# Chunk 0 of the causal attention moved into the last two steps of the memory block, and the causal block's first lead-in step dropped

## The reference, cut to what matters

```
xn = layernorm(x)                        # per token, 128 features
q, k = xn Wq + bq, xn Wk + bk            # 64 wide
A = softmax(q k^T / 8, masked to the past, inside the chunk)
x = x + A (xn (Wv Wo)) + (bv Wo + bo)    # Wv and Wo are joined into one 128 x 128 table
xn = layernorm(x); e = argmax(xn Wg + bg)
x = x + gelu(xn W1[e] + b1[e]) W2[e] + b2[e]
```

## Time and profile before

| what | value |
|---|---|
| median of three runs | 1473.49 us (1465.39 to 1476.33) |
| profiled execution, its own time | 1473.16 us |
| its span in the profile | 1471.4 us |
| TensorE busy | 1297.2 us (88% of the span) |
| VectorE, ScalarE, GpSimd busy | 1006.7, 787.0, 526.5 us |
| memory block, last two steps | 929.0 to 981.9 us of the span |
| causal block, steps -2 and -1 | 981.9 to 1026.8 us |
| causal block, from step 0 on | 1026.8 to 1239.0 us |

### The profile page before, as it was taken

One profiled execution on the slowest core, in us unless ns is written; L12 is line 12 of the kernel. 1 busy time (PEld: TensorE's weight loads), 2 busy tenths in 40 slices (PEclk: granted clock), 3 DMA queues, 4 the chain that ended last, 5 costly groups with the idle time before them and its releaser, 6 DMA issues. The chain is left out here.

```text
span 1471.4 us, 23007 instructions
## 1 busy us (share of the span) xinstructions
PE 1297.2 (88%) x7338; PEld 772.9 (53%) x7338; DVE 1006.7 (68%) x2761; ACT 787.0 (53%) x1593; POOL 526.5 (36%) x688
## 2 busy tenths in 40 slices
PE   4899999999999899944779998988999998999898
PEld 1223333333333789922355555667667676777533
DVE  7688888888885666647867876334575654666586
ACT  1377677777776205545546664223554544466555
POOL 3433443453312215258434444331221212533056
PEclk7799999999999899967889999999999999999999
DMA  5211211111111622210122234202111312000001
GB/s 151 71 35 45 56 34 45 56 48 31 56 34 52 157 47 70 55 38 23 30 65 59 60 75 99 59 13 87 62 66 63 122 59 86 9 1 2 1 22 36
DMA packets 80059, 80.05 MB, mean 54 GB/s; under 512 B 19835, under 2 KB 63947, under 8 KB 79939
## 3 DMA queue, kind: packets, MB, share of 16 engines
q1 hardware_dynamic: 76639, 72.95, 18.2%
q0 software_dynamic: 2272, 4.66, 1.4%
q10 hardware_dynamic: 1028, 0.98, 0.2%
HBM read 63.21 MB, written 13.85 MB: 52 GB/s over the span
## 5 line engine op out<-in xcount | busy, mean ns | idle before, releaser
L706 DVE TENSOR_REDUCE a_nm<-a_aps 128x1 f32<-128x512 f32 x512 | 330.0, 686 | 74.5 <-PE a_aps L426 74.5
L666 ACT ACTIVATE a_prob<-a_sps 128x512 f32<-128x512 f32 x512 | 270.0, 599 | 121.2 <-PE a_sps L439 120.7
L426 PE MATMUL a_aps<-a_K,a_Q 96*128 96x512 bf16 x512 | 190.2, 397 | 28.5 <-DMA a_K<-k_parts 27.0
L439 PE MATMUL a_sps<-a_Q,a_K 99*128 99x512 bf16 x512 | 155.9, 384 | 1.3 <-ACT a_prob L666 1.3
L1540 POOL TENSOR_TENSOR p_h<-p_sl,p_t 128x512 f32<-128x512 f32 x72 | 102.3, 1428 | 150.0 <-ACT p_sl L1744 96.9
L449 PE MATMUL a_ops<-a_prob,a_Vg 128*32 128x512 f32 x1024 | 136.9, 608 | 0.0
L426 PEld LDWEIGHTS a_aps<-a_K,a_Q 96*128 96x128 bf16 x512 | 50.3, 98 | 153.7 <-DVE a_nm L706 90.0
L2353 POOL TENSOR_TENSOR c_h<-c_h,c_G 128x512 f32<-128x512 f32 x24 | 31.9, 1334 | 171.8 <-DMA c_G<-choice_rows 128.0
L1599 PE MATMUL p_up_a<-x_normT,p1w_w 128*128 128x512 f32 x144 | 78.6, 629 | 14.5 <-ACT p_sl L1744 12.2
L104 POOL CAST a_ms<-a_mr 16x128 bf16<-16x128 f32 x32 | 9.0, 280 | 228.8 <-ACT a_mr L623 228.8
L1744 ACT ACTIVATE p_sl<-p_up_a 128x512 f32<-128x512 f32 x72 | 42.2, 592 | 77.1 <-PE p_up_b L1601 76.8
(11 more groups left out here) (649 smaller groups left out, 2742.1 us busy)
## 6 DMA issues: line engine op xcount, KB each, us to landing
c_G<-choice_rows SPq DMA_DIRECT2D x32, 512.0 KB, 5.8
p_G<-gates_by_expert SPq DMA_DIRECT2D x30, 512.0 KB, 7.6
a_Q<-q_parts SPq DMA_DIRECT2D x192, 32.0 KB
a_K<-k_parts SPq DMA_DIRECT2D x31, 96.0 KB
q_parts<-a_partsq SPq DMA_DIRECT2D x7, 384.0 KB, 2.8
k_parts<-a_partsk SPq DMA_DIRECT2D x7, 384.0 KB, 2.8
token_outputs<-m0e_y SPq DMA_DIRECT2D x39, 64.0 KB, 1.5
m0w_w<-in_L_ffn_W SPq DMA_DIRECT2D x1, 2048.0 KB, 8.6
```

The lines of the kernel that those rows point to most:

```text
L426: nc.tensor.matmul(aps[n % 3][:, :], Q[0:MAX, head, q * P:(q + 1) * P], K[0:MAX, head, :], start=True, stop=True).then_inc(a_ready, 1)
L439: nc.tensor.matmul(sps[(NS * u + k) % 3][:, :], K[0:KB, head, q * P:(q + 1) * P], Q[0:KB, head, :], start=True, stop=True).then_inc(s_read ...
L666: nc.scalar.activation(prob[u % 2][:, j, q, :], sps[n % 3][:, :], ACT.Exp).then_inc(p_done, 1)
L706: nc.vector.tensor_reduce(nm[u % 2][:, s:s + 1], aps[n % 3][:, :], AX.X, ALU.max, negate=True).then_inc(a_used, 1)
```

## The change

The start and the end of the attention of causal chunk 0 are written a second time as functions `head_*` inside the memory block, on buffers that its last two steps no longer use. In step 6: the normalisation (DVE, before j=1), its transposes (PE, behind j=1), queries and keys (j=3), the joined table, values and the joined bias (j=5), the scores behind the last pair and ahead of the `down` products, then maxima and exponentials. In step 7: the transposes of the probabilities behind j=0, the weighted sum behind j=4, the addition to the residual at j=6 and the statistics at j=8. SP issues the eight loads of attention weights in its turn for chunk 6, and ACT issues the move of the keys. POOL makes the mask and adds the bias. The tables that later chunks need live in a new object `CausalHead` that both blocks hold (four tables in the buffer that was `xn20`, so it takes the place of one).

In the causal block the steps -2 and -1 are replaced by one written-out lead-in that does the first half of chunk 1 and the second half of chunk 0's choice of experts, with 10, 4, 8 and 24 `keep_busy` matmuls where there were 10, 4, 13, 12, 8, 16, 4 and 12. Semaphores that chunk 0 would have raised are raised by hand at the start. The memory block's ScalarE ends on a load of the square-root table. From step 0 on the order of every engine is what it was. Lines left out of the diff are the loads of the other weights, the same removal in the other engines, and parameters that name the PSUM bank.

```diff
-def memory_and_swiglu(nc, net, d, mw, place, ys, rows):
+class CausalHead:
...
+        p = Scope(nc, ctx, "ch")
+        self.tables = p.sb("tables", [P, TC, D])
+        self.wqk, self.wvo, self.bc, self.mask = (self.tables[:, i, :] for i in range(TC))
+        self.qkb, self.qks = p.sb("qkb", [P, 1]), p.sb("qks", [P, 1])
...
+        xn1, xn2 = [rows, p.sb("xn11", [P, TC, D])], [head.tables, p.sb("xn21", [P, TC, D])]
...
+        hb = (ops, bps, cps)
+        xnh, xch, qkh, kTh, Vh = rz[1], l[1], az[1], sn[0], sn[1]
+        prob_of = {0: cn[0][:, 0:P], 2: cn[0][:, P:4 * P], 1: cn[1][:, 0:2 * P], 3: k[:, :]}
+        PTh = [content, cc, cs, csum]
+        wvh, woh, boh, bvh = az[0][:, 0:H], az[0][0:H, P:2 * P], az[0][:, 2 * P:3 * P], az[0][0:H, 3 * P:3 * P + 1]
+        bvbh, wvTh = rz[0][0:H, 0:P], rz[0][0:H, P:2 * P]
...
+                if c == B - 2:
+                    sp.wait_ge(x2_turned, B - 1)
+                    sp.wait_ge(phi_done, B - 1)
+                    sp.wait_ge(h_set, 2)
+                    ca = lambda n: d[f"L2_attn_{n}"]
...
+                    sp.dma_start(head.qkb[H:2 * H, :], col(ca("bk"))).then_inc(h_loaded, 16)
+                    sp.dma_start(wvh, ca("wv")).then_inc(h_loaded, 16)
+                    sp.dma_start(woh, ca("wo")).then_inc(h_loaded, 16)
+                    sp.dma_start(bvh, col(ca("bv"))).then_inc(h_loaded, 16)
+                    sp.dma_start(boh, row(ca("bo")).to_broadcast([P, D])).then_inc(h_loaded, 16)
 
...
+                    pool.wait_ge(x2_turned, B - 1)
+                    nc.gpsimd.memset(head.mask[:, :], 0.0).then_inc(h_set, 1)
+                    pool.wait_ge(h_set, 3)
+                    nc.gpsimd.affine_select(out=head.mask[:, :], in_=head.mask[:, :], compare_op=ALU.is_ge, fill=-1e11,
+                                            base=0, pattern=[[-1, P]], channel_multiplier=1).then_inc(mask_made, 1)
+                if s == B - 2:
+                    pool.wait_ge(bias_done, 1)
+                    pool.wait_ge(hx_done, 1)
+                    xt = net.x[:, 0:TC, :]
+                    nc.gpsimd.tensor_tensor(xt, xt, over_tiles(head.bc[:, :], TC), ALU.add).then_inc(hx_biased, 1)
...
+            def head_turn():
+                pe.wait_ge(r_done, B)
+                pe.wait_ge(hx_done, 1)
+                for i in range(TC):
+                    last = nc.tensor.transpose(bps[:, htok(i)], xnh[:, htok(i)], net.ident[:, :])
+                last.then_inc(hx_turned, 1)
+
+            def head_turn_values():
+                pe.wait_ge(h_loaded, 16 * head.LOADS)
+                nc.tensor.transpose(cps[0:H, 0:P], wvh, net.ident[:, :]).then_inc(wv_turned, 1)
...
+
+            def head_queries_and_keys():
+                pe.wait_ge(hxc_done, 1)
+                nc.tensor.matmul(bps[:, :], head.wqk[:, :], xch[:, :], start=True, stop=True).then_inc(hqk_ready, 1)
+
+            def head_join():
+                pe.wait_ge(wvT_done, 1)
+                nc.tensor.matmul(cps[:, P:2 * P], wvTh, woh, start=True, stop=True).then_inc(wvo_ready, 1)
+
...
+                pe.wait_ge(wvo_done, 1)
+                for i in range(TC):
+                    last = nc.tensor.matmul(cps[:, htok(i)], xch[:, htok(i)], head.wvo[:, :], start=True, stop=True)
+                last.then_inc(V_ready, 1)
+
+            def head_bias():
+                pe.wait_ge(bvb_done, 1)
+                pe.wait_ge(hqk_done, 1)
+                nc.tensor.matmul(bps[:, 0:D], bvbh, woh, start=True, stop=True).then_inc(bias_ready, 1)
+
+            def head_scores():
+                pe.wait_ge(hk_moved, 16)
+                pe.wait_ge(V_done, 1)
+                pe.wait_ge(bias_done, 1)
...
+                for q in SCORE_ORDER:
+                    bank, off = SCORE_PLACE[q]
+                    n = (q + 1) * P
+                    nc.tensor.matmul(hb[bank][:, off:off + n], qkh[0:H, q * P:n], kTh[0:H, 0:n],
+                                     start=True, stop=True).then_inc(s_ready, 1)
+
+            def head_turn_prob():
+                pe.wait_ge(p_done, 1)
+                for i in range(TC):
+                    bank, off = TURN_PLACE[i]
+                    for q in range(i, TC):
+                        last = nc.tensor.transpose(hb[bank][:, off + (q - i) * P:off + (q - i + 1) * P],
+                                                   prob_of[q][:, htok(i)], net.ident[:, :])
+                last.then_inc(p_turned, 1)
+
+            def head_weigh():
+                pe.wait_ge(PT_done, 1)
+                for q in range(TC):
+                    for i in range(q + 1):
+                        last = nc.tensor.matmul(ops[:, htok(q)], PTh[i][:, htok(q - i)], Vh[:, htok(i)],
+                                                start=(i == 0), stop=(i == q))
+                last.then_inc(w_ready, 1)
 
             join_tables()
...
+                    if s == B - 2:
+                        if j == 1:
+                            head_turn()
+                            head_turn_values()
+                        if j == 3:
+                            head_queries_and_keys()
+                            head_join()
+                        if j == 5:
+                            head_values()
+                            head_bias()
+                    if s == B - 1:
+                        if j == 0:
+                            head_turn_prob()
+                        if j == 4:
+                            head_weigh()
+                if s == B - 2:
+                    head_scores()
                 middle(s)
...
+                    if s + 2 == B - 1:
+                        nc.scalar.activation(stdh, net.stat[:, 0:TC, 1], ACT.Sqrt, bias=net.epst[:, 0:1]).then_inc(h_rooted, 1)
...
+                act.wait_ge(r_done, B)
+                nc.scalar.activation(xch[:, :], bps[:, :], ACT.Copy).then_inc(hxc_done, 1)
+                act.wait_ge(wv_turned, 1)
+                nc.scalar.activation(wvTh, cps[0:H, 0:P], ACT.Copy).then_inc(wvT_done, 1)
+
+            def head_queries_and_keys():
+                act.wait_ge(hqk_ready, 1)
+                act.wait_ge(b_scaled, 1)
+                nc.scalar.activation(qkh[:, :], bps[:, :], ACT.Identity, scale=head.qks[:, :], bias=head.qkb[:, :]).then_inc(hqk_done, 1)
+                act.wait_ge(hqk_done, 1)
+                act.dma_start(kTh[0:H, :], qkh[H:2 * H, :]).then_inc(hk_moved, 16)
+                act.wait_ge(wvo_ready, 1)
+                nc.scalar.activation(head.wvo[:, :], cps[:, P:2 * P], ACT.Copy).then_inc(wvo_done, 1)
...
+                nc.scalar.activation(Vh[:, :], cps[:, :], ACT.Copy).then_inc(V_done, 1)
+
+            def head_exponentials():
+                nc.scalar.preload_act_table(ACT.Exp)
+                act.wait_ge(nb_done, 1)
+                for q in SCORE_ORDER:
...
+                    last = nc.scalar.activation(prob_of[q], hb[bank][:, off:off + (q + 1) * P], ACT.Exp,
+                                                bias=nbh[:, q:q + 1], accum_out=sumsh[:, q:q + 1])
+                last.then_inc(p_done, 1)
+                nc.scalar.preload_act_table(ACT.Silu)
...
+                    if s == B - 2:
+                        if j == 2:
+                            head_tokens()
+                        if j == 4:
+                            head_queries_and_keys()
+                        if j == 6:
+                            head_values()
                 middle(s)
+                if s == B - 2:
+                    head_exponentials()
+            nc.scalar.preload_act_table(ACT.Sqrt)
...
+                v.wait_ge(h_rooted, 1)
+                nc.vector.reciprocal(stdh, stdh)
+                v.drain()
+                for i in range(TC):
+                    last = ts(xnh[:, htok(i)], net.x[:, i, :], net.stat[:, i, 0:1], stdh[:, i:i + 1], ALU.subtract, ALU.mult)
+                last.then_inc(hx_done, 1)
...
+            def head_biases():
+                v.wait_ge(h_loaded, 16 * head.LOADS)
+                tt(head.qkb[:, :], head.qkb[:, :], head.qks[:, :], ALU.mult).then_inc(b_scaled, 1)
+                nc.vector.tensor_copy(bvbh, bvh.to_broadcast([H, P])).then_inc(bvb_done, 1)
...
+                    v.wait_ge(s_ready, (1, 3, 3, 4)[i])
+                    dg = hb[bank][:, off + q * P:off + (q + 1) * P]
+                    tt(dg, dg, head.mask[:, :], ALU.add)
+                v.drain()
+                for q in SCORE_ORDER:
+                    bank, off = SCORE_PLACE[q]
+                    last = nc.vector.tensor_reduce(nbh[:, q:q + 1], hb[bank][:, off:off + (q + 1) * P], AX.X, ALU.max,
+                                                   negate=True)
+                last.then_inc(nb_done, 1)
+
+            def head_copy_prob(which):
+                v.wait_ge(p_turned, 1)
+                for i in which:
+                    bank, off = TURN_PLACE[i]
...
+                    last.then_inc(PT_done, 1)
+
+            def head_add():
+                v.wait_ge(p_done, 1)
```

(114 more changed lines are left out.)

186 lines of the change are left out of this document (87 added, 99 removed).

## The result

The changed kernel takes 1456.93 us, the median of 20 runs (1451.85 to 1463.59), against 1472.26 us for the kernel before in 20 runs of its own (1462.37 to 1476.33). The ratio is 0.9902, 95% interval 0.9887 to 0.9917, so 14.4 us faster (12.2 to 16.6). The profiled execution took 1460.11 us.

The account below looks back on a forecast made before the run. TensorE was taken to bound the kernel, busy 88% of the span, with the lead-in set by one chunk's latency. 1473.2 + 8.5 (memory block) - 21.5 (lead-in) = 1460.2 us, given as 1460, range 1454 to 1466.

Parts of the forecast that it names:

- Work added to TensorE: Memory steps 6 and 7: 7.78 us of moved work plus a 0.7 us wait, ending the block 8.5 us later.
- The wait: Step 6: `head_values` on TensorE waits for the joined table that ScalarE copies, 0.5 to 1.0 us, taken as 0.7.
- the joined table and the joined bias: Step 6, TensorE: one matmul each at a quarter of the four value matmuls' 0.99 us, 0.50 us together.
- The scores: End of step 6: 2.35 us on TensorE, standing where it now waits 0.83 us, so 1.52 us is added.
- The lead-in: From the engines' meeting to `weigh` of chunk 1: 23.4 us where it was 44.88, so 21.5 us earlier.
- The semaphore increments: Start of the lead-in: six on TensorE, between 0 and 0.6 us, taken as 0.3.
- The count of 24: Lead-in: 24 `keep_busy` end at 20.3 us, probabilities are ready at 19.4, so the count decides by 0.9 us.
- The clock at step 0: Under `weigh`: the low clock stays, leaving the sum unchanged; the high one would return 2.2 us.
- The first rival: Step 0: the clock stays at 2.4 GHz into it, giving 1458.0 us; chance 30%.
- longer stall: Step 6: TensorE waits 2.8 us and falls to the low clock, 2.5 us more, giving 1465.5 us; chance 9%.
- the expert weights and choices: After the lead-in: they land late, about 3 us if transfers do not overlap, giving 1463 us; chance 7%.
- VectorE and POOL did collide: Steps 6 and 7: collisions cost 1.06 us per added VectorE instruction, 1481 us if all paid; chance 4%.

Follow-up runs that it names:

- a_kb12: The changed kernel with 12 instead of 24 `keep_busy` ahead of `turn_prob` of chunk 1; 0.9903 of the kernel before.
- c_memory_only: The changed memory block with the causal block of the kernel before, so chunk 0's attention is computed twice; 1.0052 of the kernel before.
- b_fill: The kernel before with 19 instead of 12 `keep_busy` ahead of the second `turn_prob`, filling the idle 1.46 us; 0.9981 of the kernel before.

## Why the prediction was right

The forecast was 13 us faster (1460 against 1473.2) and the measurement 14.4. The mechanism, TensorE time paid in steps 6 and 7 against latency returned in the lead-in, is what the rows show. The closeness is in part luck: the two main terms came out 0.8 and 0.6 us less favourable than forecast, and the clock, on which I chose wrongly, gave 2.6 us. The terms:

- **Work added to TensorE.** 8.5 us were forecast, 9.3 measured, outside my 8.3 to 8.8. The wait was right: 0.7 forecast, 0.69 from start to start. What I sized too low are the matmuls with 64 rows, the joined table and the joined bias: 0.41 us each where I took a quarter of four value matmuls, 0.25, and the pair behind each starts its second matmul 0.1 us later (934.49 to 935.45). Queries and keys took 0.96 instead of 0.86, values 1.09 instead of 0.99. Another 0.2 us lie between the last `down` products and the meeting of the engines (11.70 instead of 11.51 us); what takes them is not shown. The scores took the place of the wait, as said. The joined table could have been read instead of guessed, since the kernel before has the same matmul in its lead-in, 0.39 us from start to start:
```profile
990.59 0.46 PE L2395 MATMUL c_ups<-c_wo,c_wvT 64*128 64x128 f32 x2 [1.01 <-ACT c_wvT L2544]
990.98 3.17 PE L75 MATMUL c_hps<-ident 128*128 128x128 f32 x26
```
- **The lead-in.** 21.5 us were forecast, 20.9 measured in the profiled pair. The semaphore increments took 0.9 us where I took 0.3. The count of 24 decided over the chain, by 1.1 us (the last exponential ended at about 1007.8, and with 12 counts the transposes came 1.05 us earlier), where I had 0.9.
- **The clock at step 0.** Here the choice was wrong in its value: I took the low clock, and all seven profiled executions with the changed lead-in or a variant of it show the high one. The first rival, 1458.0 us, is the case that came; it priced the high clock at 2.2 us, and step 0 was 2.6 us shorter, since the first pair behind `weigh` ran faster too. The reason I gave, the length of the gap, is not the cause: with both gaps the high clock came in three of three executions of `a_kb12` and `c_memory_only`, and in one of five of the kernel before. The rule of the Trainium skill that I weighed there (page "TensorE: Matmul & The Clock Gate", section "Part 4: PE-mode transpose"), that transposes don't count for the clock, is neither shown nor refuted: 3.0 us without a matmul, transposes in them, did not lower it.
- **What gain is the kernel's own.** With the same clock on both sides, a rise in the same place (4.61 us) and the high clock under `weigh`, the stretch takes 126.21 us in `b_fill`, whose filled gap does not move `weigh`, and 114.61 us in the changed kernel: 11.6 us. That is the 20.9 us of the lead-in less the 9.3 us of steps 6 and 7. With the low clock before and the high one after it is 14.2 us. The five executions of the kernel before average 128.1 us, the two of the changed kernel 114.6: 13.6 us, which the interval of 12.2 to 16.6 holds. The 2.6 us of the clock belong to the pair only as far as the kernel before falls low more often (four of five) than the changed one (none of two, and none of five for its variants).
- **The rivals.** No longer stall in step 6; the expert weights and choices were never waited for. VectorE and POOL did collide, in one place: beside POOL's addition of the bias the normalisation of chunk 0 in the new lead-in took 2.03 us, where the one ahead of it took 1.11. Timelines of VectorE, then of POOL, in the changed kernel:

```profile
989.08 1.11 DVE L2850 TENSOR_SCALAR c_xn<-x_resid,x_stat,x_rstd 128x128 f32<-128x128 f32 x4 [0.40 <-issue]
...
990.37 2.03 DVE L2904 TENSOR_SCALAR c_xn<-x_resid,x_stat,c_std 128x128 f32<-128x128 f32 x4
```
```profile
990.28 1.26 POOL L2588 TENSOR_TENSOR x_resid<-x_resid,ch_tables 128x512 f32<-128x512 f32 x1 [0.95 <-DVE c_xn L2850]
```
It cost nothing, since TensorE was at its `keep_busy` until 995.41. None of the operations added in steps 6 and 7 was slowed.

## What to carry to other kernels

A lead-in of a software pipeline is latency, and a step before it that is bound by one engine has room on all the others: moving the lead-in's first chunk there costs the bound engine's own share of it and returns the whole step. Price it as that share against the latency, 9.3 against 20.9 us here. Then read the filler matmuls again, since a count that hid a wait in the old place can become the wait in the new one.

## What the runs showed that I had not expected

- One and the same kernel ran the 20 matmuls of `weigh` in 4.64 or in 2.50 us, at 1.2 or at 2.4 GHz, from one execution to the next. Which it was went with the place where the clock rose some 40 us earlier. What puts the changes of the clock where they fall was not tried and stays open.
- Two executions of the changed kernel lay 11 us apart, all of it ahead of the change, and three quarters of it waiting of TensorE rather than slower work.
- Six semaphore increments ahead of TensorE's first matmul took about 0.9 us (0.93 from the meeting; a wait of 4.35 us with them and 3.45 without).
- A matmul over 64 rows and 128 columns cost TensorE 0.41 us between two with 128 rows, against 0.27 us for each of a run of four with 128 rows.
